# Values before scores in the steps of the second attention layer

## The reference

```python
# first layer: 16 heads of 64
h = layernorm(x, gamma, beta)
Q, K, V = h @ Wq, context @ Wk, context @ Wv
x = x + (softmax(Q K^T) * 64**-0.5 @ V) @ Wo + bo
# second layer: 16 heads of 32
xn = x * rsqrt(mean(x*x) + 1e-5) * norm_w
q = xn @ wq;  k, v = context @ wkv
q, k = rotate(q), rotate(k)          # rotary tables, then each divided by its norm
out = x + (softmax(q k^T * sqrt(32)) @ v) @ wout
```

## The kernel before, in words

| half | steps 1 to 8 |
|---|---|
| 1 | out den; out v; v; qr; kT out; kT out; qT out; out |
| 2 | den; xt xt; xt xt; qr; out; out; qT out; out |
| 3 | den; kr; kr; qr; out; out; qT out; out |
| 4 | den; kT v; v; qr; kT out; qr out; qT out; out |
| 5 | den; kr; kr; v; qT out; kT out; kT out; v out |
| 6 | den ct; qr; qr; ct ct; ct out; qT ct out; qT ct out; ct ct out |
| 7 | den; k; k; xt x4; q out; xt xt out R; xt xt out R; q out R |
| 8 | R den R; v R; v R; R; R T out R; R out R; R out R; R k q out R |

## Time and profile before

### The profile page before, as it was taken

The page is one execution under the profiler, slowest core; times in us unless marked ns, Lnnn a source line. Parts: engine busy times, 40 slices in busy tenths (PEclk is TensorE's granted clock), DMA queues, the critical chain, the costliest instruction groups (busy, mean ns, idle before and its releaser), DMA issues.

```text
span 3557.8 us, 51131 instructions
## 1 busy us (share of the span) xinstructions
PE 3207.4 (90%) x20448; PEld 1614.7 (45%) x20448; DVE 2409.5 (68%) x2805; ACT 1400.7 (39%) x1729; POOL 477.2 (13%) x221
## 2 busy tenths in 40 slices
PE   4899999889899999988989999988899999999896
PEld 2445445434345445534444445444444445445351
DVE  3566667578766666667776666667777666665776
ACT  1233333445433333344643333335453333334554
POOL 1000001233010000224300000032410000012330
PEclk7999999999999999999999999999999999999999
DMA  2000100111110101011111101101111101000001
GB/s 92 19 20 25 23 21 17 27 40 42 29 56 25 23 20 25 13 48 25 35 41 48 23 17 28 23 7 52 25 34 61 32 17 27 24 18 13 25 17 34
DMA packets 179577, 106.16 MB, mean 30 GB/s; under 512 B 82576, under 2 KB 148240, under 8 KB 179344
## 3 DMA queue, kind: packets, MB, share of 16 engines
q1 hardware_dynamic: 179344, 102.89, 10.8%
HBM read 93.39 MB, written 9.44 MB: 29 GB/s over the span
## 4 chain that ended last, share of the span: by engine, by line
PE 72%; DVE 13%; issue 5%; ACT 4%; POOL 3%; DMA 2%; SPq 1%; DVEq 0%; ACTq 0%; POOLq 0%
PE o_acc L652 18%; PE scores L640 15%; PE work L678 12%; PE work L674 11%; PE work L698 7%; PE work L610 5%; DVE tile_max L776 3%; DVE acc L795 3%; PE work L692 2%; ACT probs L725 2%; POOL inv L906 2%; DVE q_low L867 1%; DVE k_low L867 1%; ACT q_high L740 1%; PE work L682 1%
## 5 line engine op out<-in xcount | busy, mean ns | idle before, releaser
L725 ACT ACTIVATE probs<-scores 128x1024 f32<-128x1024 f32 x1024 | 996.4, 1023 | 724.0 <-PE scores L640 661.3
L795 DVE TENSOR_TENSOR acc<-acc,probs 128x1024 f32<-128x1024 f32 x768 | 990.9, 1311 | 29.8 <-ACT probs L725 8.4
L776 DVE TENSOR_REDUCE tile_max<-work 128x2 f32<-128x1024 f32 x512 | 625.8, 1222 | 313.8 <-PE work L610 313.6
L652 PE MATMUL o_acc<-probs,v_tok 128*64 128x512 f32 (+1 forms) x4096 | 788.9, 622 | 0.1
L906 POOL TENSOR_TENSOR inv<-sumsq,power 128x16 f32<-128x16 f32 x64 | 223.1, 3486 | 2344.8 <-DVE sumsq L858 2344.3
L698 PE MATMUL work<-wo,o_sum 128*128 128x512 f32 x768 | 423.6, 638 | 40.5 <-issue 38.1
L877 DVE TENSOR_TENSOR resid<-work,resid 128x512 f32<-128x512 f32 x384 | 262.9, 685 | 177.1 <-PE work L698 176.8
L640 PE MATMUL scores<-q_high,k_high 32*128 32x512 f16 (+1 forms) x2048 | 314.0, 398 | 69.4 <-DVE q_low L867 41.4
L610 PE MATMUL work<-k_high,q_high 64*128 64x512 f32 x1024 | 246.1, 473 | 143.1 <-DVE tile_max L776 87.7
L652 PEld LDWEIGHTS o_acc<-probs,v_tok 128*64 128x64 f32 (+1 forms) x4096 | 166.6, 124 | 347.1 <-issue 318.4
L640 PE MATMUL scores<-q_high,k_low 32*128 32x512 f16 (+1 forms) x2048 | 308.4, 390 | 0.0
(11 more groups left out here) (73 smaller groups left out, 2630.3 us busy)
## 6 DMA issues: line engine op xcount, KB each, us to landing
recip<-rows_dram SPq DMA_DIRECT2D x384, 64.0 KB, 2.1
wq<-in_L_xattn_Wq_dram SPq DMA_DIRECT2D x32, 256.0 KB, 3.0
stage<-in_x_dram SPq DMA_DIRECT2D x8, 1024.0 KB, 7.7
resid<-in_x_dram SPq DMA_DIRECT2D x8, 1024.0 KB, 5.2
wo<-in_L_xattn_Wo_dram SPq DMA_DIRECT2D x32, 256.0 KB, 2.7
out_dram<-resid SPq DMA_DIRECT2D x8, 1024.0 KB, 4.8
wk<-in_L_xattn_Wk_dram SPq DMA_DIRECT2D x32, 192.0 KB, 2.6
wv<-in_L_xattn_Wv_dram SPq DMA_DIRECT2D x32, 192.0 KB, 3.2
```

Source lines behind the costliest of these rows:

```text
L652: mm = pe.matmul(o_acc[h * d:(h + 1) * d, :], v_tok[par][:, kt, h * d:(h + 1) * d], probs[:, unit_slot(t, n, kt, h // 2), h % 2, :], start ...
L725: act.activation(probs[:, no % RING, :, :], scores[:, unit_banks(t, n, kt, u), :], ACT.Exp, scale=(1.0, float(D1) ** 0.5 / QK_SCALE ** 2)[ ...
L776: dve.tensor_reduce(tile_max[:, qt, :, n:n + 1], work[:, 0:G0, :], AX.X, ALU.max, negate=True).then_inc(dve_freed, 1)
L795: dve.tensor_tensor(a[:, heads, :], before, probs[:, unit_slot(t, n, kt, u), :, :], ALU.add).then_inc(add_ok, 1)
```

## The change

In every step with one block, which is every step of the second layer, the scores of the next block are issued behind the values of the current block and not ahead of them. Since all engines share `run`, ScalarE's exponentials of the next block now stand behind its copy of `o_acc` as well; for VectorE, GpSimd and SyncE the order stays. Steps of the first layer, the two steps marked late in each batch entry and the opening step stay as they are.

```diff
             for at, st in enumerate(PLAN):
                 after = PLAN[at + 1] if at + 1 < len(PLAN) else None
-                if after is not None and not st.late:
+                values_first = len(st.kts) == 1
+                if after is not None and not st.late and not values_first:
                     for kt in after.kts:
                         scored(after.t, after.n, kt)
                 for e in st.first:
...
                 for kt in st.kts:
                     blocks(st.t, st.n, kt)
+                if after is not None and values_first:
+                    for kt in after.kts:
+                        scored(after.t, after.n, kt)
                 for e in st.fill:
```

## The result

| | before | after |
|---|---|---|
| median of four runs, taken together | 3567.01 (3560.77 to 3573.24) | 3636.64 (3632.27 to 3640.06) |
| profiled execution, its span | 3559.66, 3557.8 | 3635.95, 3634.2 |
| mean granted clock | 0.972 | 0.970 |

The ratio is 1.0195, with a 95% interval of 1.017 to 1.0219: the change makes the kernel slower by 70 us in the medians, 76.4 in the spans. Forecast were 3627 and 55.6. A step is measured from the start of its scores to the start of the next ones. A stage or a half is measured from its first instruction, which is its scores before and its values in the changed order (the window of the last two halves goes from scores in both).

The account below looks back on a forecast made before the run. TensorE was taken to bound the kernel, standing still most in the second layer. Entries 1 to 3 cost 36.9 us, the last 22.7, clock -4: 55.6 us, giving 3615 profiled and 3627 median; range 3600 to 3650, 8 in 10 3592 to 3658.

Parts of the forecast that it names:

- halves 1 to 4, all entries, clock included: Second-layer halves 1 to 4: losses in den, out and half 2's steps, less 4.0 us per stage for filled waits, clock -4.
- half 5, four: Half 5 of each second-layer stage: 1.00 us for its den step and 1.9 us for steps 5 to 7.
- half 6, four: Half 6 of each second-layer stage: exposed values in short steps cost 2.1 us in entries 1 to 3, 3.3 in the last.
- halves 7 and 8, last entry, and the end: Last entry: 15 steps without a long fill go from 47.89 to 62.25 us, +14.4; at the very end -1.0.
- The order itself: Second-layer steps: values now follow the fill; a step loses 1.00 us for fills up to 1.18, nothing from 2.18 up.
- Waits hidden and filled: Second-layer stages: some losses vanish in waits for VectorE; values moved into the `q_low` waits give -1.0 us per half, -4.0.
- the clock's term: Steps behind the `q_low` waits run less at half clock: -4 us taken, with a bound of -15 if all ten go.
- Half 8: Half 8 of entries 1 to 3, with row maxima: step 1 loses 1.8 us and the last step 1.5 us per entry.
- its two terms: Half 8: 1.8 us from adjacent maxima and fill in step 1; 1.5 us from first-layer scores following the wait that ended at 963.94.
- ScalarE: ScalarE's queue: its `o_acc` copy costs nothing; evacuations wait for exponentials ending 1.0 us later, but TensorE waits then anyway in short steps.
- the rival: Short steps: pauses drop TensorE's clock, a third of some 100 run at half clock, 63 us more, 3690 in all; chance 0.10.
- the offset: Whole kernel: the median of the runs stands 11.5 us above the profiled execution, which raised the forecast from 3615 to 3627.

Follow-up runs that it names:

- The shorter exponentials: Only one of two heads computed in each second-layer exponential, on the kernel before and on the changed kernel: 3543.82 (0.9946) with the old order, 3561.95 (0.9987) with the new.

## Why the prediction was right, and where its sizes were off

The sum of the forecast beside the spans, with the same stretches in both:

| | forecast | measured |
|---|---|---|
| halves 1 to 4, all entries, clock included | 12.1 - 4 = 8.1 | -1.3, -0.4, +0.6, +5.7 = 4.6 |
| half 5, four | 4 x 2.9 = 11.6 | 2.9 each, 11.5 |
| half 6, four | 3 x 2.1 + 3.3 = 9.6 | 2.3, 0.4, 0.4, 4.0 = 7.1 |
| halves 7 and 8, entries 1 to 3 | 3 x 4.3 = 12.9 | 10.7, 11.8, 11.7 = 34.1 |
| halves 7 and 8, last entry, and the end | 14.4 - 1.0 = 13.4 | 20.4 + 1.0 (values now ahead) - 2.1 = 19.3 |
| sum | 55.6 | 76.6 (spans 76.4; the first layer and the opening -0.3) |

**The order itself: right.** 4.15 us in a step with one out, kr unchanged, 115.8 us of waits by the values where some 100 were forecast, and half 5 to a tenth of a microsecond. The shorter exponentials tie the loss to them.

**Waits hidden and filled: right, and mis-sized in the clock's term.** The `q_low` wait fell from 41.4 to 12.8 us, with the values ahead of it, as this timeline of after has it where half 1 of the first entry ends:

```profile
689.23 0.68 DVE L871 TENSOR_TENSOR q_low<-work,q_high 128x512 f16<-128x512 f32 x1
...
690.00 0.40 PE L644 MATMUL scores<-q_high,k_high 32*128 32x512 f16 x4 [0.76 <-DVE q_low L871]
```

The pause is 0.76 us, and the steps behind the sixteen pauses are 3.3 us over their 4.15, where before had 15.4 over 3.15. The clock thus gave back some 12 us, against the 4 taken (the bound was 15).

**Half 8: mis-sized, and by the most.** 6.3 to 7.4 us an entry in place of 3.3 (1.8 + 1.5), some 11 of the 21 us that the sum lacks. The runs do not say which of its two terms was short.

**ScalarE: the step that failed.** I wrote that evacuations wait for exponentials that end 1.0 us later, but that "in short steps TensorE waits then anyway". The xt steps are not short: three of them in half 7 paid the 1.0 us in full, some 3.0 us per entry and 8.9 in all. The forecast had put this at nothing.

**The clock in short steps: the rival had a piece of it.** The forecast named a clock under 0.95 in the last two halves as a sign against it, and it was 0.85 there. The timeline of after in the empty steps of half 7:

```profile
3548.87 0.61 PE L644 MATMUL scores<-q_high,k_high 32*128 32x512 f16 x4
...
3552.87 1.93 PE L656 MATMUL o_acc<-probs,v_tok 128*32 128x512 f32 x8 [2.11 <-ACT probs L729]
3554.73 0.61 PE L644 MATMUL scores<-q_high,k_high 32*128 32x512 f16 x4
```

A step takes 5.86 us at half clock, scores 0.61 for 0.40 and values 1.93 for 1.07 (3548.87 to 3560.69, two empty steps, has a granted clock of 0.50). Four of the six empty steps took 4.99 to 5.96 us, and in each half the first step with an out behind them was still drawn in (4.83 and 5.01 us); the later ones, whose pause is 1.05 to 1.2 us, are at 4.15 again. It came to 7 us, and the rival's 63 did not come. Two sentences of that rival do not hold as written. A standstill of 2.39 us is not always enough: in two entries of before full clock followed it. And not every short step is busy less than all stretches that held the clock: one with an out is busy 2.97 of 4.15 us, where an empty step of before held it with 1.97 of 3.15.

**Median and execution.** The forecast set the median 11.5 us above the profiled execution. With four runs each it is 7.4 before and 0.7 after, so the total came within 10 us of the forecast although the spans' sum was 21 us too small. That half of the error was hidden by the offset is luck.

## What to carry to other kernels

Between two products that wait for the same other engine, keep all independent work that there is: moving the consumer next to its producer takes its own length out of the cover. Issue it early only where a longer wait for something else follows, as at the half ends here; done there alone it gained 18 us, where done in every step it lost 70. Of every engine that also frees buffers, ask what in its queue now stands ahead of that.

## What the runs showed of the hardware

- In the last two halves of after, TensorE stood still for 2.1 to 2.4 us in each empty step, and four of the six took 4.99 to 5.96 us and not 4.15, with half clock in them; the steps with an out, except the first behind them, held 1.00. The Trainium skill, page "TensorE: Matmul & The Clock Gate", section "A second HAM failure mode: psum-queue depth-cycling", tells of frequent micro-idles between groups of products that make the clock swing. Here pauses of 1.05 to 1.2 us in every step did not, those of 2.1 us did, though not in every execution to the same extent (64.83 to 68.28 us for these halves in four of them).
- Useless products kept the clock in two places: 6.9 us less in a window of 68 (3.5 in that whole kernel), and 7 us less in the whole kernel at the half ends.
- One late item had a second cost: the pause itself and then a step at half clock, 4.62 in place of 3.15 us, so that a wait of 2.39 us costs 3.9. It is not certain: the same wait was followed by 3.15 us in two of four entries.
